# Three units become GpSimd blocks: 23 units and 26 GpSimd blocks, and a new order of periods

## The reference

```
h = max(layernorm(x), 0)
agg = segment_sum(h[src], dst) / max(number of edges into the node, 1)
g = relu(agg @ Wg + h @ Ws + bg)        # 128 -> 128
g = tanh(g @ W1 + b1)                   # 128 -> 512
g = tanh(g @ W2 + b2)                   # 512 -> 512
out = x + (g @ W3 + b3)                 # 512 -> 128
```

## Time and profile before

| what | value |
|---|---|
| median of three runs | 1314.92 us |
| span of the profiled execution, first to last instruction | 1311.4 us |
| the runs lie above that span by | 3.2 to 5.4 us |
| TensorE busy | 1190.5 us (91%) |
| VectorE busy | 1067.0 us (81%) |
| GpSimd busy, 744 gathers of 973 ns in it 724.2 us | 746.2 us (57%) |
| ScalarE busy | 617.0 us (47%) |

### The profile page before, as it was taken

The page is one execution under the profiler, slowest core; times in us unless marked ns, Lnnn a source line. Parts: engine busy times, 40 slices in busy tenths (PEclk is TensorE's granted clock), DMA queues, the critical chain, the costliest instruction groups (busy, mean ns, idle before and its releaser), DMA issues.

```text
span 1311.4 us, 28364 instructions
## 1 busy us (share of the span) xinstructions
PE 1190.5 (91%) x10092; PEld 942.7 (72%) x10092; DVE 1067.0 (81%) x2050; ACT 617.0 (47%) x1299; POOL 746.2 (57%) x793
## 2 busy tenths in 40 slices
PE   0238889999999999999999999999999999999998
PEld 0215667777777778788777777877777787787777
DVE  8899998878879878878878897888798798788640
ACT  5724445435435535534535454454364355355332
POOL 4265545566566566666655666666566566566520
PEclk9759999999999999999999999999999999999999
DMA  9752431442342343244144414414424423542410
GB/s 239 234 144 91 100 98 37 113 117 51 108 116 86 73 117 107 53 115 117 44 111 101 113 47 115 119 44 115 115 64 96 115 88 72 113 105 57 119 29 12
DMA packets 88716, 128.14 MB, mean 98 GB/s; under 512 B 45251, under 2 KB 71193, under 8 KB 84233
## 3 DMA queue, kind: packets, MB, share of 16 engines
q1 hardware_dynamic: 64773, 77.52, 21.8%
q0 software_dynamic: 23808, 48.81, 15.4%
HBM read 106.68 MB, written 13.15 MB: 91 GB/s over the span
## 4 chain that ended last, share of the span: by engine, by line
PE 78%; DVE 10%; ACT 5%; issue 4%; DMA 2%; POOL 1%; DVEq 0%; SPq 0%; POOLq 0%
PE banks L863 24%; PE banks L809 20%; PE banks L825 10%; PE banks L880 7%; PE banks L734 7%; PE banks L846 3%; PE banks L837 2%; PE banks L782 2%; DVE arena L1498 2%; ACT arena L1057 2%; ACT dense L1119 2%; PE banks L840 1%; DVE arena L1508 1%; DMA arena<-unit_codes 1%; DVE mean_rows L1537 1%
## 5 line engine op out<-in xcount | busy, mean ns | idle before, releaser
L660 POOL DMA_INDIRECT ring<-h_table,idx_all x744 | 724.2, 973 | 483.6 <-issue 220.8
L1136 ACT CAST arena<-banks 128x512 f16<-128x512 f32 (+1 forms) x650 | 355.4, 581 | 136.6 <-PE banks L809 130.8
L863 PE MATMUL banks<-dense,w 128*128 128x256 f32 (+1 forms) x1568 | 415.6, 382 | 1.6
L809 PE MATMUL banks<-xin,arena 128*128 128x256 f16 x2548 | 351.2, 273 | 25.5 <-DVE arena L1498 24.2
L809 PEld LDWEIGHTS banks<-xin,arena 128*128 128x128 f16 x2548 | 235.2, 98 | 102.5 <-issue 27.3
L863 PEld LDWEIGHTS banks<-dense,w 128*128 128x128 f32 x1568 | 264.3, 190 | 37.7 <-ACT dense L1119 10.7
L1508 DVE TENSOR_TENSOR arena<-node,banks 128x768 f16<-128x768 f16 x208 | 187.6, 963 | 7.1 <-PE banks L825 6.9
L1498 DVE TENSOR_SCALAR arena<-arena,code_ptr 128x768 f16<-128x768 f16 (+1 forms) x416 | 165.6, 460 | 8.7 <-PE banks L809 5.9
L825 PE MATMUL banks<-arena 64*128 64x257 f16 x2548 | 154.4, 272 | 7.3 <-DVE arena L1508 6.8
L734 PE MATMUL banks<-ring,onehot 128*128 (+1 forms) x828 | 156.4, 275 | 0.3
L1126 ACT ACTIVATE dense<-banks,b2c 128x256 f32<-128x256 f32 (+1 forms) x196 | 93.7, 478 | 128.1 <-PE banks L863 128.1
(11 more groups left out here) (121 smaller groups left out, 859.5 us busy)
## 6 DMA issues: line engine op xcount, KB each, us to landing
arena<-unit_codes SPq DMA_DIRECT2D x26, 1568.0 KB, 8.1
ring<-h_table,idx_all POOLq DMA_INDIRECT x744
xblk<-in_x_dram SPq DMA_DIRECT2D x48, 128.0 KB
out_dram<-dense SPq DMA_DIRECT2D x48, 128.0 KB
xin<-in_x_dram SPq DMA_DIRECT2D x4, 1232.0 KB, 15.7
h_table<-xin SPq DMA_DIRECT2D x4, 1232.0 KB
own_pair<-h_table SPq DMA_TRANSPOSE x98
w<-in_L_gnn_W_dram SPq DMA_DIRECT2D x1, 1024.0 KB, 6.2
```

The lines of the kernel that those rows point to most:

```text
L660: nc.gpsimd.indirect_dma_start(out=ring_tiles[:, t % RING, 0:2 * D], out_offset=None, in_=table, in_offset=bass.IndirectOffsetOnAxis(ap=id ...
L809: mm = nc.tensor.matmul(to, wide_l[:, piece % WSLOTS, k, j, :], tab[:, row_of(g, j), :], start=(j == 0), stop=(j == 1))
L863: mm = nc.tensor.matmul(l3_ps[c][:, 0:w], w2[:, q, c * P:(c + 1) * P], h2T[:, q, 0:w], start=(q == 0), stop=(q == HC - 1))
L1136: nc.scalar.copy(unit_msgs[:, 2 * pr:2 * pr + wide_of, 0:2 * D], unit_ps[pr % 2][:, 0:wide_of * 2 * D].rearrange("p (g d) -> p g d", d=2 * ...
```

## The change

`PB` goes from 23 to 26: three units become GpSimd blocks, so there are 23 units and 26 GpSimd blocks, 52 steps in place of 46, and 840 gathers in place of 744. Only period 1 is without a GpSimd block. Behind periods 6, 10, 14 and 18 comes a new stretch (`extra_block`) with one GpSimd block, two steps for the next, and no unit. `LOT_NS` goes from 1385 to 1000, so that `pace` hands over room at shorter intervals on its written clock. In period 1, where VectorE used to do one step's mean and one 0/1 matrix, it now does both means and three 0/1 matrices.

```diff
--- before.py
+++ after.py
...
-LOT_NS = 1385
+LOT_NS = 1000
 BLK = 256
 SUB = 128
 W = 18
 REACH = 22
-PB = 23
-UNITS_ALONE = (1, 2, 13)
+PB = 26
+EXTRA_BEHIND = (6, 10, 14, 18)
...
-    PERIODS, ORDER = [((), [])], []
+    PERIODS, EXTRA, ORDER, pool = [((), [])], {}, [], 0
     for n in range(1, UNITS):
-        pool = n - sum(alone <= n for alone in UNITS_ALONE)
         if n == 1:
             PERIODS.append(((0, 1), [PB]))
-        elif n in UNITS_ALONE:
-            PERIODS.append(((), [PB + n - 1]))
         else:
-            PERIODS.append(((2 * pool, 2 * pool + 1), [pool - 1, PB + n - 1]))
+            PERIODS.append(((2 * pool + 2, 2 * pool + 3), [pool, PB + n - 1]))
+            pool += 1
         ORDER += PERIODS[n][1]
+        if n in EXTRA_BEHIND:
+            EXTRA[n] = ((2 * pool + 2, 2 * pool + 3), pool)
+            ORDER.append(pool)
+            pool += 1
     LAST_POOL, LAST_UNIT = len(ORDER), len(ORDER) + 1
...
+        def behind(n):
+
+            return EXTRA[n][1] if n in EXTRA else PERIODS[n + 1][1][0]
...
+                if n in EXTRA:
+                    finish_block(PLACE[EXTRA[n][1]])
...
             def end_period(n):
 
-                following = PERIODS[n + 1][1][0]
+                following = behind(n)
                 if is_unit(following):
                     sum_unit(n, range(NP))
                 else:
+                    ahead = WSLOTS if n == 1 else 0
+                    sum_unit(n, range(ahead))
                     turn(PLACE[following])
-                    sum_unit(n, range(NP - 1))
+                    sum_unit(n, range(ahead, NP - 1))
                     layer1(following, PLACE[following])
                     sum_unit(n, [NP - 1])
+
+            def extra_block(n):
+
+                steps, block = EXTRA[n]
+                k = PLACE[block]
+                following = PERIODS[n + 1][1][0]
+                leads = {}
+
+                def beside_layer3(slot):
+                    if slot < W // 3:
+                        sum_tiles(steps[0], leads[0], range(3 * slot, 3 * slot + 3))
+                    if slot == 9:
+                        leads[1] = begin_sums(steps[1])
+                    if slot > 9:
+                        sum_tiles(steps[1], leads[1], range(3 * (slot - 10), 3 * (slot - 9)))
+
+                def beside_layer4(slot):
+                    if slot == 3:
+                        turn(PLACE[following])
+
+                layer2(block, k)
+                leads[0] = begin_sums(steps[0])
+                layer3(block, k, beside_layer3)
+                layer4(k, n + 2, beside_layer4)
+                layer1(following, PLACE[following])
...
             for n in range(1, UNITS):
-                if n in UNITS_ALONE:
+                if n == 1:
                     period_alone(n)
                 else:
                     period(n)
+                if n in EXTRA:
+                    extra_block(n)
...
+            def begin_block(m):
+
+                take_rows(PLACE[m])
+                after_layer1(m, PLACE[m])
+
             def end_period(n):
 
-                following = PERIODS[n + 1][1][0]
-                if not is_unit(following):
-                    take_rows(PLACE[following])
-                    after_layer1(following, PLACE[following])
+                if not is_unit(behind(n)):
+                    begin_block(behind(n))
+
+            def extra_block(n):
+
+                _steps, block = EXTRA[n]
+                after_layer2(block, PLACE[block])
+                after_layer3(block, PLACE[block])
+                begin_block(PERIODS[n + 1][1][0])
...
                 match_codes(n, [6, 7])
-                if n == 1:
-                    finish(0)
-                if n == 2:
-                    finish(1)
+                finish(steps[0])
                 rank_edges(n + 1)
                 spread_ranks(n + 1, range(UCH))
-                if n == 1:
-                    make_onehot(1)
-                if n == 2:
-                    make_onehot(2)
+                make_onehot(steps[1])
                 match_nodes(n, range(WSLOTS))
-                if n == 2:
-                    make_onehot(3)
                 residual(PLACE[unit])
                 add_own(PLACE[unit] + 1)
+                finish(steps[1])
                 match_nodes(n, range(WSLOTS, NP))
+                make_onehot(steps[0] + 2)
+                make_onehot(steps[1] + 2)
                 begin_unit(n + 1)
+
+            def extra_block(n):
+
+                steps, block = EXTRA[n]
+                k = PLACE[block]
+                add_own(k + 1)
+                step(steps[0])
+                step(steps[1])
+                residual(k)
...
-                if n in UNITS_ALONE:
+                if n == 1:
                     place_edges(n + 1)
                     count_groups(n + 1)
```

More of the change, by code:

```diff
@@ L115, in gnn_program @@
     UC = IC * P - UT0
-    assert D == P and UNITS - 1 - len(UNITS_ALONE) == PB - 1 and UNITS_ALONE[0] == 1 and UNITS_ALONE[-1] < UNITS - 1
+    assert D == P and UNITS - 2 + len(EXTRA_BEHIND) == PB - 1 and 1 < EXTRA_BEHIND[0] and EXTRA_BEHIND[-1] < UNITS - 1
     assert TP * ROWS_OF + LAST_OF == N and ODD and TC >= 5 and 2 * HI <= P and ROWS_OF % 2 == 0 and ROWS % 2 == 0 and TP == P - 1
```

## The result

The changed kernel takes 1264.87 us (median of 4 runs, 1264.43 to 1268.35). The kernel before, run beside it, takes 1314.76 (1312.19 to 1316.81). The ratio is 0.9624, with a 95% interval of 0.9606 to 0.9642: 49.9 us faster. The forecast was 1261.5, with a range of 1256 to 1274. The profiled span is 1263.2 us, 5.3 above the forecast span of 1257.9.

What follows compares the result with a forecast made beforehand. TensorE was taken to bound the kernel. Span: 1311.4 - 121.45 (removed periods) + 68.4 (stretches) + 2.7 (period 1) - 3.2 (last gather's wait) = 1257.9 us; time about 1261.5 us, range 1256 to 1274.

Steps and rivals of the forecast that it cites:

- The mechanism: Whole kernel: TensorE sets the period; three periods, 121.45 us, go and four stretches, 68.4 us, come.
- GpSimd keeps up: Gathers: 1.273 us each back to back against 1.298 allowed per cycle, so no wait, margin only 2%.
- (a): Rival: GpSimd becomes the bound, each cycle taking 160 (x - 1.298) more; 1266 to 1282 us, chance 0.14.
- Rival (c): VectorE's match_codes hold gathers for their whole length: cycle 223.9 us, +65 us in all, 1326 us, chance 0.02.
- The extra stretch: Each added stretch, on TensorE alone: 17.1 us net including waits of 0.35, 0.6 and 0.1, four times 68.4.
- two steps are 36 x 0.11 = 4.0: Within each added stretch: the sums of its two steps on TensorE take 4.0 us, 0.11 each.
- The clock fell only after 3 us without work: TensorE's clock in the stretches: no single wait there is above 0.6 us, so no slowdown was expected.
- (b): Rival: stretches cost more by waits on VectorE and low clock, +10 to 16 us; 1270 to 1278, chance 0.07.
- Regular periods of 47.6: Periods of a unit and a GpSimd block: still 47.6 us each by the first pairs, as before.
- Period 1: Unit 2's pairs near 164.4, 1.1 us later; TensorE stands some 4 us, low clock adds 1.6: together +2.7 us.
- -3.2 us: Last period: the 1.78 us wait for the last gather and about 1.4 us of low clock go.
- The step from span to time: Whole run: median lay 3.5 us above the span, so span 1257.9 becomes about 1261.5 us.

Runs made afterwards that it cites:

- Experiment 6: Changed kernel with its stretches bunched behind periods 6, 8, 10 and 12: 1288.92 us, ratio 0.9812 to the kernel before.
- Experiment 3: Changed kernel with its stretches moved to behind periods 5, 10, 15 and 20: 1261.71 us, ratio 0.9601 to the kernel before.
- experiment 4: Changed kernel with VectorE making step 3's 0/1 matrix in period 2, not at the end of period 1: 1259.83 us, ratio 0.9588 to the kernel before.
- experiment 2: The changed kernel run once more, unedited, on another run's chip beside the kernel before: 1264.07 us, ratio 0.9618.
- experiment 5: Changed kernel with SyncE issuing a GpSimd block's store ahead of the next block's transposing loads: 1261.98 us, ratio 0.9605 to the kernel before.
- Experiment 1: Kernel before with only LOT_NS changed from 1385 to 1000: 1313.25 us against 1313.12, ratio 0.9998.
- the joined kernel: Changed kernel, stretches behind 5, 10, 15, 20, later matrix, earlier store, four sums a slot in stretches' second steps: 1672.36 us, ratio 1.1651, on a slow chip.

## Why the prediction was right

**The mechanism** held in each part. Three periods of 121.5 us went, four stretches came, and TensorE stayed the bound at full clock. The removed periods need no correction.

**GpSimd keeps up** was right for its stated reason: 1.262 to 1.271 us a gather in the four longest runs of the first trace (and up to 1.283 in others) for 1.273, no wait for the ring. The real margin is 2 to 3%, since the cycles are 209.6 us and not 207.7. Experiment 6 shows what lies behind the margin, at the price that (a)'s rule gives.

**Rival (c)**, that `match_codes` hold the gathers for their whole length, is refuted. The gathers between 614.95 and 775.83 ran beside the `match_codes` of three units and more and lost some 0.03 us each above 0.94 + 0.30. By (c) that cycle had needed 223.9 us; it took 209.6. By the Trainium skill, SBUF — State Buffer, section "Who interferes with whom", GpSimd and a VectorE instruction in a two-port mode lock the shared ports against each other, and whichever issues second blocks fully. So (c) is the upper end of that rule, the case in which it is always the gather that waits. The trace after shows no full block on either side. 147 of the 840 gathers ran partly beside a `match_codes` and took 1015 ns on average, the others 961; a `match_codes` of 128x768 that began while a gather ran took 432 ns, one with no gather beside it 414.

**The extra stretch** was mis-sized by 3%: 17.6 us net on average for 17.1. Its named waits are within 0.14 us. The term that was short is "two steps are 36 x 0.11 = 4.0", and only for two of the four: the stretches behind 10 and 18 cost 16.97 and 17.05, as forecast. In those behind 6 and 14 the first step's groups of three sums take 0.51 to 0.67 us for 0.33, some 1.1 us in all. Experiment 3 takes these groups back to 0.33, and the stretches behind 4, 9, 14 and 19 have them in all four. That the register instructions are the cause is the reading that fits, but the last sums of step 23 have them too and lose nothing; what hides them there is not shown.

**"The clock fell only after 3 us without work"**, the argument against (b), is a misreading. The earlier trace rows has a wait of 1.78 us, and the clock of the earlier trace rows fell right there. In the trace of before it also fell to 0.50 from 676.9 to 680.3, behind waits of 1.84, 0.55 and 0.56 us, and in experiment 4 behind 2.0 us. Behind waits of 2.4 and 2.6 us in period 0 of the changed kernel (first trace and experiment 2) it did not. So no safe length of wait can be read from these rows; in the stretches, where no wait is above 0.56 us, the clock stayed up.

**"Regular periods of 47.6"** was the largest error, 3.45 of the 5.3 us. I carried the mean of the earlier trace rows over, though a period's place numbers and thus the moments at which stores, broadcasts and loads meet in SyncE's queue change with the order. Periods 7, 11 and 20 alone hold 2.8 of the 3.45, and TensorE's waits in them are the late 0/1 matrices of experiment 5, which takes back 2.4 us. How often VectorE waits for the store (15 times against 11) doesn't give the size: in experiment 3 it is 17 times, 48.7 us, and the regular periods are 47.73. What counts is where in the period the wait falls.

**Period 1** was near: TensorE stood 3.95 us for "some 4", the clock fell to 0.62 behind it, and the pairs began 0.8 earlier than forecast. The loss in period 2 was put at 1.6 and came out at 2.5; with the same stall it was 2.3 in experiment 2, 2.9 in 5 and 3.5 in 3. Most of the spread is how long the clock stayed low. The windows of the changed kernel, and of experiment 3 from the first pairs on:

```profile
164.70:168.10 3.40, 3.40 (x13) 2.23 (x14) 3.17 (x12) 1.23 (x3) 2.07 (x2) 0.50 0.08 19
164.23:169.50 5.27, 5.27 (x21) 3.61 (x22) 5.00 (x16) 1.76 (x3) 1.89 (x2) 0.50 0.05 12
```

At half speed 3.4 us lose 1.7 and 5.27 lose 2.6, and the 5.9 us of experiment 5 lose 3.0, all of its 2.9. The rest, 0.8 and 0.9 us, stands for the most part within the unit's last sums, as in periods 7, 11 and 20, and is gone in experiment 5. Experiment 4 gives the price of stall and clock together: 2.6 us at unit 3's pairs, and 4.0 counted from unit 1's pairs, behind its low clock in period 0.

**"-3.2 us"** for the last gather's wait is there in the trace (70.46 us of tail for 73.95). The term was small by 0.3: 3.4 us at 0.50 lose 1.7, not 1.4. Experiment 1 shows that it can't be had by the interval alone: the tail is shorter, the median the same.

**The step from span to time** was 3.5 us by one profiled execution, and 1.7 after. Every other execution whose span is known took 1.8 to 1.9 us more than its own span. So 3.5 was mostly the distance of the profiled execution from the median, and it hid a third of the error by luck. The change saved 49.9 us where the forecast had 53.4.

## What to carry to other kernels

An engine's share on the page doesn't say whether it can take more; a cycle's count by its back-to-back interval does, and here it was right to 1%, down to a margin of 2 to 3%. When work is moved into a place of its own, what was hidden beside other work can show up (here, most likely, register instructions between matmuls): take the duration of such a row from a place where nothing stands beside it. And when a plan changes the order of everything, a regular period's mean is no constant: the waits for rare transfers (a store behind loads in one queue) are what changes in it. One profiled execution gives the span, not its place among the runs: compare spans with spans.

## What was not expected of the hardware

- In a step with two register instructions ahead of each of its first 16 sums, the first groups of three take 0.51 to 0.69 us for 0.33, in every stretch of every trace that begins with such a step. The same instructions ahead of the last 8 sums of a stretch's second step cost nothing: three take 0.34 us, and four in a row, in the joined kernel, 0.45.
- 127 gathers one after another keep 1.267 us, and 435 keep 1.274, beside a VectorE that is busy four fifths of the time with f16 `tensor_scalar` and `tensor_tensor`.
- The clock fell to half behind waits of 1.78 and 2.0 us in two traces, and stayed up behind others of 2.0 to 2.6.
- On one chip three programs took 1649 to 1656 us that took 1260 to 1289 elsewhere, with TensorE, VectorE and ScalarE standing at once 71 times in the trace read; the kernel before took 1414 there, and 1438 on a second such chip, for 1313. A comparison made on one such chip would have called a change of -4% one of +17%.
